# GpSimd takes two of a head's eight squarings in the first pass of a cross attention

## What is computed

```
qk     = Q @ K.T                       # 256 x 4096 for each of 16 heads
scores = qk / sqrt(16)
mean_sim = scores.mean(axis=(-2, -1))
max_sim  = scores.max(axis=-1).mean(axis=-1)
probs    = softmax(scores, axis=-1)
entropy_proxy = var(probs, axis=-1, ddof=1).mean(axis=-1)
t      = exp(clip(mlp([mean_sim, max_sim, entropy_proxy])))     # one number for each head
out    = softmax(qk / (2 * t)) @ V
```

## Time and profile before

| What | Before |
|---|---|
| median of 3 runs | 1524.52 us |
| lowest and highest | 1521.98, 1524.65 us |
| the profiled execution's own time | 1520.61 us |
| its span in the trace | 1518.8 us |
| busy over the span | PE 1241.2, DVE 961.5, ACT 853.6, POOL 384.3 us |
| first pass, first to last exponential | 54.7 to 308.1 us |

### The profile page before, as it was taken

One profiled execution on the slowest core, in us unless ns is written; L12 is line 12 of the kernel. 1 busy time (PEld: TensorE's weight loads), 2 busy tenths in 40 slices (PEclk: granted clock), 3 DMA queues, 4 the chain that ended last, 5 costly groups with the idle time before them and its releaser, 6 DMA issues. The chain is left out here.

```text
span 1518.8 us, 25358 instructions
## 1 busy us (share of the span) xinstructions
PE 1241.2 (82%) x8423; PEld 729.2 (48%) x8423; DVE 961.5 (63%) x1633; ACT 853.6 (56%) x1179; POOL 384.3 (25%) x149
## 2 busy tenths in 40 slices
PE   7677777739999689899578889888888889746798
PEld 3243343424443466788324445444444444424587
DVE  6898898931011665522339898998898899735321
ACT  3699999949998244333136565656565565313210
POOL 1000000000000040000036666766676666500000
PEclk9899999969999689899759998999999899757899
DMA  7854545457551510244578877877787878142040
GB/s 263 271 154 117 127 100 117 106 107 137 110 104 26 179 68 1 70 152 152 193 249 281 286 255 260 294 276 262 252 279 259 282 268 270 62 139 77 0 166 7
DMA packets 97047, 257.50 MB, mean 170 GB/s; under 512 B 11193, under 2 KB 41305, under 8 KB 85466
## 3 DMA queue, kind: packets, MB, share of 16 engines
q1 hardware_dynamic: 96992, 256.79, 54.5%
HBM read 165.31 MB, written 91.92 MB: 169 GB/s over the span
## 5 line engine op out<-in xcount | busy, mean ns | idle before, releaser
L1975 POOL TENSOR_TENSOR xb_row<-xb_row,w_mask 128x1024 f32<-128x1024 f32 x128 | 359.7, 2820 | 400.6 <-DVE xb_row L1996 400.2
L2005 DVE CUSTOM_DVE_ANT_0 xb_row<-xb_row,xb_minus 128x1024 f32<-128x1024 f32 x128 | 222.0, 1734 | 0.1
L1996 DVE TENSOR_TENSOR xb_row<-xb_cont_ps,xb_row 128x1024 f32<-128x1024 f32 x128 | 155.8, 1217 | 59.4 <-PE xb_cont_ps L1820 58.8
L1935 ACT COPY xb_turned<-xb_turn_ps 128x1024 f32<-128x1024 f32 x64 | 64.8, 1012 | 214.0 <-PE xb_turn_ps L1849 214.0
L1820 PE MATMUL xb_rel_ps<-xb_kk,xb_qq 32*128 32x512 f32 x512 | 169.7, 744 | 10.8 <-ACT xb_out L1924 9.5
L1849 PEld LDWEIGHTS xb_turn_ps<-_ident,xb_row 128*128 128x128 f32 x1024 | 134.3, 163 | 72.2 <-issue 69.8
L1849 PE MATMUL xb_turn_ps<-_ident,xb_row 128*128 128x128 f32 x1024 | 159.7, 307 | 8.5 <-ACT xb_turned L1935 2.4
L1820 PE MATMUL xb_cont_ps<-xb_kk,xb_qq 32*128 32x512 f32 x512 | 165.1, 724 | 0.0
L1924 ACT COPY xb_out<-xb_rel_ps 128x1024 f32<-128x1024 f32 x128 | 129.8, 1014 | 53.9 <-PE xb_rel_ps L1820 51.6
L567 DVE TENSOR_REDUCE xa_stats<-xa_b_ps 128x1 f32<-128x1024 f32 x128 | 153.1, 1220 | 8.9 <-PE xa_b_ps L466 8.7
L828 ACT ACTIVATE xa_probs<-xa_psT,xa_t_now 128x1024 f32<-128x1024 f32 x128 | 141.2, 1114 | 25.6 <-PE xa_psT L787 25.4
(11 more groups left out here) (363 smaller groups left out, 1833.9 us busy)
## 6 DMA issues: line engine op xcount, KB each, us to landing
xb_row<-rel_scores SPq DMA_DIRECT2D x128, 512.0 KB, 5.2
rel_scores<-xb_out SPq DMA_DIRECT2D x32, 1024.5 KB, 4.9
rel_scores<-xb_out SPq DMA_DIRECT2D x32, 1024.0 KB, 4.8
b_e_w<-in_L_ffn_e_w SPq DMA_DIRECT2D x32, 513.0 KB, 3.5
w_w<-in_L_ffn_w SPq DMA_DIRECT2D x24, 512.0 KB, 7.4
xa_k<-first_parts SPq DMA_DIRECT2D x24, 384.0 KB, 5.0
value_rows<-xa_values SPq DMA_DIRECT2D x16, 544.0 KB, 6.1
xb_kk<-key_blocks SPq DMA_DIRECT2D x17, 512.0 KB, 6.3
```

The lines of the kernel that those rows point to most:

```text
L1975: nc.gpsimd.tensor_tensor(row[:, u, at:at + SUB], row[:, u, at:at + SUB], mask[:, t, half * HALF + at:half * HALF + at + SUB], ALU.mult).t ...
L1996: nc.vector.tensor_tensor(row[:, u, at:at + SUB], cont_ps[:], row[:, u, at:at + SUB], ALU.add).then_inc(s["cont_out"], 1)
L2005: nc.vector.tensor_tensor_reduce(out=row[:, u, at:at + SUB], in0=row[:, u, at:at + SUB], in1=minus[:, t, half * HALF + at:half * HALF + at ...
```

## The change

Quarters 2 and 5 of each head are squared by POOL. ACT squares 0, 4 and 6, DVE 1, 3 and 7. [...] `keep` on DVE then first reduces the two 64-column rows into `stats`, waits for that, and copies the statistics as before. A semaphore `pool_squared` is raised by the last of POOL's sums; the exponential of quarter 6 and that of quarter 1 of the next head wait for it, and so does `keep`.

```diff
+            FOLDS, FOLDED = 4, QUARTER // 16
+            folded = f.sb(inner, "folded", [P, 2, 2, FOLDED])
...
+            ACT_SQUARES, DVE_SQUARES, POOL_SQUARES = (0, 4, 6), (1, 3, 7), (2, 5)
+
+            def squares_kept(eng, h, u):
+                before, u = (h, u - 4) if u >= 4 else (h - 1, u + 4)
+                for mine, done in ((ACT_SQUARES, "even_squared"), (DVE_SQUARES, "odd_squared"),
+                                   (POOL_SQUARES, "pool_squared")):
+                    if u in mine:
+                        eng.wait_ge(s[done], len(mine) * before + mine.index(u) + 3)
...
-                    act.wait_ge(s["odd_squared" if u % 2 else "even_squared"], NU // 2 * h + u // 2 + 1)
+                    squares_kept(act, h, u)
...
-                            square(it, c, 2 * j)
+                            if 2 * j in ACT_SQUARES:
+                                square(it, c, 2 * j)
                             product_out(it, c, j)
...
+                    dve.wait_ge(s["pool_squared"], len(POOL_SQUARES) * (h + 1) + 2)
                     dve.wait_ge(s["exp_done"], NU * (h + 2))
+                    first, last = POOL_SQUARES
+                    nc.vector.tensor_reduce(stats[:, c % 2, 2, first:last + 1:last - first], folded[:, c % 2], AX, ALU.add
+                                            ).then_inc(s["unfolded"], 1)
+                    dve.wait_ge(s["unfolded"], h + 1)
                     nc.vector.tensor_scalar(stats_all[:, bass.ds(h, 1)].rearrange("p h k u -> p (h k) u"), stats[:, c % 2],
                                             1.0, None, ALU.mult).then_inc(s["kept"], 1)
...
-                            if j > 0:
+                            if 2 * j - 1 in DVE_SQUARES:
                                 square(it, c, 2 * j - 1)
+                            elif j > 0:
+                                pass
...
+            @block.gpsimd
+            def _(pool):
+                pool.sem_inc(s["pool_squared"], 2)
+
+                def square(it, c, u):
+                    h, n = HPB * it + c, POOL_SQUARES.index(u)
+                    pool.wait_ge(s["exp_done"], NU * (h + 1) + u + 1)
+                    pool.wait_ge(s["pool_squared"], len(POOL_SQUARES) * h + n + 2)
+                    if n == 0:
+                        pool.wait_ge(s["kept"], h + 1)
+                    steps, width = FOLDS * (len(POOL_SQUARES) * h + n), QUARTER
+                    nc.gpsimd.tensor_tensor(rest[:], exps[:, u % 4], exps[:, u % 4], ALU.mult).then_inc(s["pool_product"], 1)
+                    for k in range(FOLDS):
+                        pool.wait_ge(s["pool_product"], steps + k + 1)
+                        width //= 2
+                        if k < FOLDS - 1:
+                            nc.gpsimd.tensor_tensor(rest[:, 0:width], rest[:, 0:width], rest[:, width:2 * width], ALU.add
+                                                    ).then_inc(s["pool_product"], 1)
+                        else:
+                            nc.gpsimd.tensor_tensor(folded[:, c % 2, n], rest[:, 0:width], rest[:, width:2 * width], ALU.add
+                                                    ).then_inc(s["pool_squared"], 1)
+
+                with pool.Fori(0, NB) as it:
+                    for c in range(HPB):
+                        for u in POOL_SQUARES:
+                            square(it, c, u)
```

More of the change, by code:

```diff
@@ L375, in cross0 @@
             values = f.sb(inner, "values", [P, 2, H // 2, CPH, DV])
+            FOLDS, FOLDED = 4, QUARTER // 16
+            folded = f.sb(inner, "folded", [P, 2, 2, FOLDED])
             s = {n: f.sem("b_" + n) for n in ("scored", "projected", "product_out", "min_ready", "exp_done", "even_squared",
-                                              "odd_squared", "kept", "ones_set", "squares_begun", "edges_stored")}
+                                              "odd_squared", "kept", "ones_set", "squares_begun", "edges_stored",
+                                              "pool_product", "pool_squared", "unfolded")}
             keys_stored = [f.sem(f"b_keys_stored{b}") for b in range(2)]
@@ L522, in square @@
                     act.wait_ge(s["exp_done"], NU * (h + 1) + u + 1)
-                    act.wait_ge(s["even_squared"], NU // 2 * h + u // 2 + 2)
+                    act.wait_ge(s["even_squared"], len(ACT_SQUARES) * h + ACT_SQUARES.index(u) + 2)
                     act.nop()
@@ L572, in square @@
                     dve.wait_ge(s["exp_done"], NU * (h + 1) + u + 1)
-                    dve.wait_ge(s["odd_squared"], NU // 2 * h + u // 2 + 2)
+                    dve.wait_ge(s["odd_squared"], len(DVE_SQUARES) * h + DVE_SQUARES.index(u) + 2)
                     dve.sem_inc(s["squares_begun"], 1)
@@ L580, in keep @@
                     h = HPB * it + c
-                    dve.wait_ge(s["odd_squared"], NU // 2 * (h + 1) + 2)
-                    dve.wait_ge(s["even_squared"], NU // 2 * (h + 1) + 2)
+                    dve.wait_ge(s["odd_squared"], len(DVE_SQUARES) * (h + 1) + 2)
+                    dve.wait_ge(s["even_squared"], len(ACT_SQUARES) * (h + 1) + 2)
+                    dve.wait_ge(s["pool_squared"], len(POOL_SQUARES) * (h + 1) + 2)
                     dve.wait_ge(s["exp_done"], NU * (h + 2))
+                    first, last = POOL_SQUARES
+                    nc.vector.tensor_reduce(stats[:, c % 2, 2, first:last + 1:last - first], folded[:, c % 2], AX, ALU.add
+                                            ).then_inc(s["unfolded"], 1)
+                    dve.wait_ge(s["unfolded"], h + 1)
                     nc.vector.tensor_scalar(stats_all[:, bass.ds(h, 1)].rearrange("p h k u -> p (h k) u"), stats[:, c % 2],
```

## The result

The changed kernel takes 1552.91 us (median of 4 runs, 1548.63 to 1561.59), beside 1523.25 us for the kernel before: a ratio of 1.0206, with a 95% interval of 1.0158 to 1.0255. It is 2.1% slower, some 30 us, where 22.5 us were forecast. Each ratio further on is to executions of the kernel before from the same session, whose medians were 1522.56 to 1525.42 us. The profiled execution took 1552.69 us, 32.1 more than that of before.

A forecast was written before the change was run, and what follows sets the result against it. It took the 3.89 us leg through VectorE's square and minimum as the bound, ScalarE's 3.83 close behind. Heads going from 15.56 to 16.93 add 22 us, the end 0.5: 1524.5 + 22 + 0.5 = 1547 us, range 1535 to 1568.

The forecast's parts named there:

- the exclusion: Two-input SBUF operations of VectorE and GpSimd side by side: one waits for the whole of the other.
- its own case: First pass: VectorE's squares wait for GpSimd, the copy does not; 16.93 us a head, 22 us slower, chance 0.55.
- rival A: VectorE's copy of a head's statistics also waits for GpSimd's product: 1559 to 1565 us, chance 0.22.
- The legs: From one odd exponential to the next, through VectorE's square and the next odd minimum: 3.89 us a pair of quarters.
- the two loops: Per pair: exponential, VectorE's square, minimum, exponential at 3.89 us, against ScalarE's own order at 3.83.
- rival B: Squares read one tensor for both inputs, so nothing waits: 15.50 us a head, 1523.5 us, chance 0.11.
- The loop of VectorE and ScalarE: The four legs of a head with contention, 4.92 + 3.83 + 3.89 + 3.89 = 16.53 us.
- The leg from 3 to 5: Between exponentials 3 and 5; grows from 3.89 to 4.92 us as quarter 3's square waits for GpSimd's product.
- the leg from 7 to 1: From exponential 7 of the head before to exponential 1; stays at 3.89 us.
- The loop over GpSimd: GpSimd's chains of quarters 2 and 5, then ScalarE from exponential 1 to 2 and hand-overs: 16.93 us a head, binding.
- a hand-over to GpSimd: From an exponential's start to GpSimd's start on it: between 1.26 and 1.49 us, taken as 1.49.
- rival D: GpSimd's chains longer, small folds 0.72 us each: 18.3 us a head, 1568 us, chance 0.08.

The follow-up runs named there:

- e1: Changed kernel with VectorE's copy of the statistics written as a reduction over an axis of one element: 1535.98 us, ratio to before 1.0088.
- e4: Changed kernel with GpSimd only waiting and signalling, squares and folds of quarters 2 and 5 left out: 1521.28 us, ratio to before 0.998.
- e6: Kernel before, with both minima of a pair placed ahead of VectorE's square: 1514.41 us, ratio to before 0.9931.
- e3: Changed kernel with the copy as a reduction and VectorE's three squares replaced by one-input plain sums: 1520.0 us, ratio to before 0.9961.
- e5: e1 with a quarter's buffer released by GpSimd's product instead of its folds: 1536.39 us, ratio to before 1.0084.
- e8: Changed kernel with copy as reduction, both minima before the square, and buffer released by GpSimd's product: 1506.51 us, ratio to before 0.9884.
- e11: e8 with quarters 1 and 2 on GpSimd in place of 2 and 5; VectorE squares 3, 5, 7: 1500.53 us, ratio to before 0.9858.

## Why the prediction was right

The direction, the range (1535 to 1568) and the exclusion as its cause held; 30 us came where 22.5 were forecast. The loop that was to bind did not, and that the measured 1552.9 us lies in the forecast's own range (1541 to 1554) is luck: its own case would have cost 13 us (e1), and rival A added 17. Step by step:

- **The legs were right, ScalarE's side of them too long.** The gain of the removal alone, forecast as 0.06 a head, was 0.03 to 0.07 (e4), as the sum of a larger gain and two losses that the forecast did not have. But the two loops are not 0.06 apart: I took 0.57 for every eviction, where half of them cost 0.47, and e6 shows 14.95 a head for ScalarE alone. I also took 15.56 for all heads before; those of the first iteration take 15.3.
- **Exclusion was right, also for two inputs that are the same tensor** (rival B falls: squares of 1.67 us in e1, none over 1.22 with one input in e3). The loop of VectorE and ScalarE, 16.53 by my sum, looks like the 16.45 measured in the first heads, but its parts do not. The leg from 3 to 5 is 4.48 us in head 2, for my 4.92, and the leg from 7 to 1 is 4.44, for my 3.89: I had the square of 7 meet the folds and did not put that into this sum. The two errors cancel, which is luck.
- **The loop over GpSimd did not bind.** I held it for the bound with 16.93. GpSimd's product takes 1.90 us, not the 2.34 that I took from a row with two different tensors. That takes 0.9 us from the loop, 16.0, below 16.45, and e5 shows that ScalarE does not wait for it. By this the forecast's own case would have been 1.15 a head in the first heads, and e1, where the squares are held and the copy is not, is 13 us slower than before rather than 22.
- **Rival A happened, in 11 of 16 heads.** I gave it 0.22 and placed the copy 4.11 us after exponential 1, the product 4.21. Measured: the product at 4.14 to 4.15 and the copy at 4.02 in the first iteration, but at 4.20 from head 4 on. There the copy's address comes from a register (12 of the 16 copies), and 0.15 us lie between the reduction and the copy where I put 0.03. This is the term that was mis-sized, and it decided: 17 of the 30 us. The condition that I gave for A, a hand-over to GpSimd under 1.38 us, was not what decided: it was 1.43 to 1.49. By the Trainium skill, page "SBUF — State Buffer", section "Who interferes with whom", a VectorE copy in its two-port mode and a GpSimd instruction exclude each other, and whoever issues first has the ports for the whole instruction. The trace agrees for a product that starts 0.02 us or more ahead of the copy of 24 numbers: the copy lasts 1.87 to 1.91 us. In which mode the copy runs, no row shows. The same section says that a reduction never contends on this chip; in e1 it doesn't, 178 ns beside the product.
- **A held copy costs more than its 1.7 us.** Heads 5, 6, 9, 10, 13 and 14 take 18.7 to 19.2 us, 2.2 to 2.3 more than the same heads of e1. In head 6 the steps 3-4 and 4-5 hold 1.35 of that (the square of 3 meets only a fold, so step 4-5 is shorter), and 7-0 and 0-1 hold 0.9, where TensorE's product runs at a granted clock of 0.50 to 0.59. Heads 7 and 11, with the clock at 1.00, show step 7-0 without this. The forecast had no term for the clock.
- **Small folds** (rival D falls) were as costed: 0.456 us for 128 columns in e3, 0.320 for 64, for my 0.45 and 0.31.

## What to carry to other kernels

An engine at 99% of a stage need not be its bound: follow one unit of work around the engines and compare that leg with the busy time, then look for an operation in the leg that only stands there by order; moving one line was worth 8 to 10 us here, and handing work to an idle engine paid only together with that and with the earlier release of the buffer (e8, e11). Work for GpSimd beside VectorE is costed with the exclusion, for every VectorE operation that can be caught and not only for the large ones: a copy of 24 numbers ahead of a minimum cost more (17 us, with the clock that fell behind it) than the squares of every head (13). Where two engines' starts are within a tenth of a microsecond of each other, choose the order or the form of the operation so that the race cannot matter.

## What the runs showed of the hardware that I had not expected

GpSimd multiplies 1024 columns of a tensor with itself in 1.90 us (32 instructions, 1.893 to 1.936), and two different tensors in 2.33 at least; that the shared input is what makes the difference was not tested. The winner of the exclusion is settled by hundredths of a microsecond, and not strictly by the recorded starts: the copy is free where it starts up to 0.006 us behind the product (head 4 of the changed kernel; the product then takes 1.94 us in place of 1.89), and waits for the whole product from 0.02 us behind. And where GpSimd's fold is ready 0.08 us after its product, a VectorE square that has been waiting goes first each time: the fold takes 2.12 in place of 1.27.
